# Base, expert and router products as one of 656 columns, with a new order of the stages

## The chip, the cores and the metric

The kernel runs on one core of a Trainium2 chip. The metric is the device time of one launch, in microseconds (us); lower is better.

## The reference

The input x has 128 batch rows of 32 x 512 floats. A block of four parts works on it: a mixing of the 32 rows of each batch entry by weights that depend on a condition, causal attention with grouped keys, a grouped convolution over the 512 positions, and a feed-forward part that adds eight low-rank experts, weighed by a router, to a base product.

```python
def _L0_cond_ref(x, embedding, W0, b0, W1, b1, W2, b2, weight, bias_k):
    ...
    out = jnp.einsum('boi,bih->boh', agg_w, x) + agg_b[:, :, None]
    return out
def _L0_attn_ref(x, Wq, Wk, Wv, Wo):
    ...
    scores = jnp.einsum('bkgqd,bkmd->bkgqm', qg, k) / np.sqrt(HEAD_DIM)
    scores = jnp.where(causal, scores, -jnp.inf)
    attn = jax.nn.softmax(scores, axis=-1)
    ...
    return out @ Wo
def _L0_ffn_ref(x, base_W, base_b, router_W, router_b, A, B, expert_map):
    ...
    base_out = jnp.einsum('btd,od->bto', x, base_W) + base_b
    logits = jnp.einsum('btd,nd->btn', x, router_W) + router_b
    probs = jax.nn.softmax(logits, axis=-1)
    topk_p, topk_i = jax.lax.top_k(probs, E)
    mapped = expert_map[topk_i]
    onehot = (mapped[..., None] == jnp.arange(E)).astype(x.dtype)
    w = jnp.einsum('btk,btke->bte', topk_p, onehot)
    h = jnp.einsum('btd,erd->bter', x, A)
    lora = jnp.einsum('bter,eor->bto', h * w[..., None], B) * SCALING
    return base_out + lora
...
    x = x + _L0_attn_ref(_L0_cond_ref(x, ...), ...)
    x = x + _L0_ffn_ref(_L0_cond2_ref(x, ...), ...)
```

## The kernel before

Four batch rows make a group of 128 partitions; there are G = 32 groups. All engines run one program of steps t, one step for each group, and in each step every engine works on groups of different age: `live(t)` guards the attention of group t, `live(t - 1)` its output projection, the convolution and the router's input, `live(t - 2)` the base product and the experts, `live(t + 1)` the mixing of the next group. The first steps and the last are written out (`peeled`), the middle ones are one loop. Each engine takes its instructions in the order in which `steps` writes them; between engines there are only semaphores. So the order is a hand-written one, and a wait in front of an instruction holds up all that follows on that engine.

The names that the text uses, in the order of TensorE (PE) in a step: `qkv` (12 products of 512 columns for the queries, 12 of 256 for keys and values), `project` (12 of 512, the output projection of the group before), `transpose_qk`, `base` (12 of 512 into PSUM bank 6), `transpose_hw` and `lora` (the expert part: 3 of 512, added into bank 6), `scores`, `conv` (12 products of 128 columns, in full fp32, two records each in the trace), `transpose_p`, `mix` (bank 6), `values` (reads what ScalarE copies out of the transposes, tile `prT`, by the name `raw` in the trace), `heads` (12 of 256 columns, of which 143 are used: 128 for the experts' inner products, 15 for the router), `transpose_o`. Three products stand where one would do mathematically, since each fp32 operand is split into a high and a low part of type fp32r: high x high, high x low, low x high. In the trace the 36 products of `qkv` and `project` and the 12 of `heads` all carry line L375, that of the helper `product`.

VectorE (DVE) does the rope, the key tile (`keys`, L974), x1 = attention + input (L1016), half of the copies by phase for the convolution (L282; ScalarE does the others), the row maximum and its subtraction for the softmax (L983, L985, in two halves h), the output sum (L1042), the convolution's bias (`zs`, L1048), the mixing's bias (`ys`, L1060), the router (`route`, `route2`, 12 small instructions) and the normalisation of the attention (L992, L994). ScalarE (ACT) makes the high parts and the exponentials, GpSimd (POOL) the low parts `z_lo` (L786) and `y_lo`, and x1 + bias (`x1b`, L800).

Of the kernel before, what the change touches and what calls it, by code (L numbers as in the profile page):

```python
# [34 lines left out]
NAR = 256  # L35
# [51 lines left out]
def build(nc, x, cond, fside, cW0, cb0, cW1, cb1, cW2, cb2, cweight, cbias, Wq, Wk, Wv, Wo,  # L87
          convw, convc, baseW, baseb, routerW, routerb, loraA, loraB, emap, const, out):
    with ExitStack() as ctx:
# [17 lines left out]
        base_hi = sb("base_hi", [P, PH, D], F32R)  # L107
        base_lo = sb("base_lo", [P, PH, D], F32R)
        ar_hi = sb("ar_hi", [P, PH, NAR], F32R)
        ar_lo = sb("ar_lo", [P, PH, NAR], F32R)  # L110
# [149 lines left out]
        ffn_ps, out_sb = sem("ffn_ps"), sem("out_sb")  # L260
# [8 lines left out]
        def iterate(eng, steps):  # L269

            for t in range(-1, 3):
                steps(t)
            with eng.Fori(3, G - 1) as t:
                steps(t)
            for t in range(G - 1, G + 2):
                steps(t)
# [11 lines left out]
        def _(sp):  # L288
# [55 lines left out]
            def steps(t):  # L344
# [4 lines left out]
                if live(t - 2):  # L349
                    wait(sp, out_sb, t - 1)  # L350
                    sp.dma_start(group(out_g, t - 2), outS).then_inc(out_st, 16)
# [5 lines left out]
            for t in range(-1, 3):  # L357
                steps(t)
            with sp.Fori(3, G - 2) as t:
                steps(t)  # L360
            for t in range(G - 2, G + 2):
                steps(t)
# [3 lines left out]
        def _(pe):  # L366
# [97 lines left out]
            def mix(u):  # L464
# [10 lines left out]
            def qkv(t):  # L475
                pe.wait_ge(y_hi_sb, t + 1)
                pe.wait_ge(y_lo_sb, t + 1)

                wait(pe, sx_sb, 2 * t)
                y = [(y_hi[:, c * P:(c + 1) * P], y_lo[:, c * P:(c + 1) * P]) for c in range(KC)]  # L480
                if peeled(t, 0):
# [4 lines left out]
                        ).then_inc(q_ps, 1)  # L486
                if peeled(t, 0):
# [19 lines left out]
            def transpose_hw(u):  # L507
                pe.wait_ge(hw_sb, u + 1)
                nc.tensor.transpose(ps[:, 7, 0:P], hw[:, :, :].rearrange("p e r -> p (e r)"), ident).then_inc(hwT_ps, 1)

            def base(u):
                z = [(z_hi[:, j, :], z_lo[:, j, :]) for j in range(PH)]
                n = 0
                for j in range(PH):
                    for a, b in ((z_hi, base_hi), (z_hi, base_lo), (z_lo, base_hi)):
                        mm(ps[:, 6, :], a[:, j, :], b[:, j, :], start=(n == 0), stop=False)  # L516
                        n += 1
# [13 lines left out]

            def lora(u):
                pe.wait_ge(hwT_hi_sb, u + 1)
                pe.wait_ge(hwT_lo_sb, u + 1)
                mm(ps[:, 6, :], hwT_hi[:, :], lora_hi[:, :], start=False, stop=False)  # L535
                mm(ps[:, 6, :], hwT_hi[:, :], lora_lo[:, :], start=False, stop=False)  # L536
                mm(ps[:, 6, :], hwT_lo[:, :], lora_hi[:, :], start=False, stop=True).then_inc(ffn_ps, 1)  # L537
# [18 lines left out]
            def values(t):  # L556

                wait(pe, zs_sb, t)
# [8 lines left out]
            def heads(u):  # L567

                pe.wait_ge(z_hi_sb, u + 1)
                pe.wait_ge(z_lo_sb, u + 1)  # L570
                z = [(z_hi[:, j, :], z_lo[:, j, :]) for j in range(PH)]
                product(ps[:, 7, 0:NAR], z, [(ar_hi[:, j, :], ar_lo[:, j, :]) for j in range(PH)]).then_inc(ar_ps, 1)

            def transpose_o(t):
                pe.wait_ge(on_sb, t + 1)

                wait(pe, ys_sb, t + 2 if live(t + 1) else 0)
                for b in range(NB):
                    last = nc.tensor.transpose(ps[:, 6, b * P:(b + 1) * P], on[:, b, :], ident)  # L579
# [518 lines left out]
```

## Time and profile before

| | |
|---|---|
| median of 3 runs | 747.89 us (747.72 to 748.15) |
| profiled execution | 748.08 us, of which the span of the trace is 746.1 us |
| TensorE busy | 711.7 us, 95% of the span |
| VectorE busy | 543.9 us, 73% |
| ScalarE busy | 272.5 us, 37% |
| GpSimd busy | 147.6 us, 20% |
| DMA | 47 GB/s over the span |

The span is the time from the first to the last instruction on the slowest (here the only) core. Busy time of TensorE is that of its matmul records, which overlap; so a busy share near 100% tells that the engine is rarely idle, and the distance from one start to the next tells what a matmul costs. PEld is TensorE's weight load, which runs beside the matmuls.

### The profile page before, as it was taken

The page shows a single profiled execution, that of the slowest core. Times are in us where ns is not written, and L with a number is a line of the kernel's source. Part 1 is how long each engine was busy: PE and PEld are TensorE (multiplying, and loading weights), DVE is VectorE, ACT ScalarE, POOL GpSimd, SP SyncE. Part 2 cuts the span into 40 slices and gives each one's busy share as a digit, 9 for nine tenths or more (in the row PEclk, how much of TensorE's full clock was granted, in tenths as well). Part 3 has the DMA queues.
Part 4 walks back from the last instruction along what each step waited for, and adds up shares of the span by engine and source line. Part 5 has one row for each costly group of instructions (what it writes and reads, how often), then busy time and mean ns, then how long its engine had stood idle before and what let it go on. Part 6 is the DMA issues. An engine that isn't in the chain of part 4 may idle for free.

```text
span 746.1 us, 13077 instructions
## 1 busy us (share of the span) xinstructions
PE 711.7 (95%) x4478; PEld 628.5 (84%) x4510; DVE 543.9 (73%) x1424; ACT 272.5 (37%) x635; POOL 147.6 (20%) x116
## 2 busy tenths in 40 slices
PE   5879999999999999999999999999999999999985
PEld 4578888888888888888888888888889888888874
DVE  5457787777778777777877777788777777877763
ACT  4135433333443333344333323433333344333331
POOL 5232201222221122222102222210122222012211
PEclk9979999999999999999999999999999999999999
DMA  7751100111110011111100111110011111001000
GB/s 189 169 242 29 43 17 27 42 42 42 42 42 31 15 38 42 42 42 42 40 16 28 42 42 42 42 42 14 28 42 42 42 42 42 19 23 42 29 29 29
DMA packets 27392, 35.43 MB, mean 47 GB/s; under 512 B 11651, under 2 KB 13347, under 8 KB 26998
## 3 DMA queue, kind: packets, MB, share of 16 engines
q1 hardware_dynamic: 26374, 34.88, 15.1%
q10 hardware_dynamic: 864, 0.14, 0.1%
q0 software_dynamic: 144, 0.28, 0.1%
q8 instruction: 6, 0.10, 0.1%
q14 instruction: 4, 0.03, 0.0%
HBM read 26.36 MB, written 8.93 MB: 47 GB/s over the span
## 4 chain that ended last, share of the span: by engine, by line
PE 82%; ACT 7%; POOL 5%; DVE 3%; issue 2%; DMA 0%; POOLq 0%; SPq 0%; DVEq 0%
PE ps L375 37%; PE ps L516 11%; PE ps L545 11%; PE ps L528 8%; POOL z_lo L786 5%; ACT raw L644 4%; PE ps L552 2%; PE ps L579 2%; ACT z_hi L644 2%; PE ps L504 2%; PE ps L562 1%; PE ps L535 1%; PE ps L536 1%; PE ps L537 1%; PE ps L526 1%
## 5 line engine op out<-in xcount | busy, mean ns | idle before, releaser
L786 POOL TENSOR_TENSOR z_lo<-raw,z_hi 128x512 fp32r<-128x512 f32 x32 | 40.8, 1274 | 561.1 <-ACT z_hi L644 561.1
L545 PEld LDWEIGHTS ps<-convW,x1ph 128*128 128x128 f32 x768 | 90.6, 192 | 2.8
L545 PE MATMUL ps<-convW,x1ph 128*128 128x128 f32 x768 | 90.9, 275 | 0.0
L644 ACT ACTIVATE x1ph<-raw 32x128 f32<-32x128 f32 x256 | 78.9, 308 | 32.0 <-DVE raw L1016 29.4
L375 PE MATMUL ps<-wqkv_hi,y_hi 128*128 128x512 f32 (+1 forms) x256 | 90.5, 353 | 0.0
L375 PE MATMUL ps<-wqkv_hi,y_lo 128*128 128x512 f32 (+1 forms) x256 | 87.4, 341 | 0.0
L375 PE MATMUL ps<-wqkv_lo,y_hi 128*128 128x512 f32 (+1 forms) x256 | 87.3, 341 | 0.0
L644 ACT ACTIVATE qk_t<-ps 128x512 f32<-128x512 f32 x32 | 19.1, 598 | 177.5 <-PE ps L505 177.5
L811 DVE TENSOR_TENSOR oT_lo<-ps,oT_hi 128x512 fp32r<-128x512 f32 x32 | 22.1, 692 | 70.8 <-ACT oT_hi L644 70.8
L528 PE MATMUL ps<-qk_t 128*128 128x256 f32 x256 | 66.7, 383 | 4.4 <-issue 2.8
L723 ACT ACTIVATE raw<-raw 128x512 f32<-128x512 f32 x64 | 40.3, 630 | 76.5 <-DVE raw L985 76.5
L562 PE MATMUL ps<-vm,raw 128*128 128x68 f32 x512 | 61.1, 273 | 0.3 <-ACT raw L644 0.3
L562 PEld LDWEIGHTS ps<-vm,raw 128*128 128x128 f32 x512 | 60.1, 193 | 0.6 <-DVE raw L1048 0.6
L282 DVE COPY x1ph<-raw 32x128 f32<-32x128 f32 x256 | 55.6, 217 | 3.0
L528 PEld LDWEIGHTS ps<-qk_t 128*128 128x128 f32 x256 | 49.3, 193 | 9.2 <-issue 0.3
L958 DVE TENSOR_TENSOR network<-ps,cst 128x512 f32<-128x512 f32 x64 | 31.5, 492 | 33.4 <-PE ps L375 33.0
L375 PEld LDWEIGHTS ps<-wqkv_hi,y_hi 128*128 128x128 f32 x256 | 49.3, 192 | 7.6 <-issue 1.5
L375 PEld LDWEIGHTS ps<-wqkv_lo,y_hi 128*128 128x128 f32 x256 | 49.1, 192 | 6.2
L375 PEld LDWEIGHTS ps<-wqkv_hi,y_lo 128*128 128x128 f32 x256 | 48.9, 191 | 6.2
L516 PE MATMUL ps<-base_hi,z_hi 128*128 128x512 f32 x128 | 53.0, 414 | 0.0
L375 PE MATMUL ps<-wo_hi,oT_hi 128*128 128x512 f32 x128 | 49.8, 389 | 1.6 <-DVE oT_lo L811 1.6
L516 PE MATMUL ps<-base_hi,z_lo 128*128 128x512 f32 x128 | 50.5, 395 | 0.0
(168 smaller groups left out, 1530.1 us busy)
## 6 DMA issues: line engine op xcount, KB each, us to landing
xm<-x SPq DMA_DIRECT2D x32, 256.0 KB, 2.6
xr<-x SPq DMA_DIRECT2D x32, 256.0 KB, 2.8
out<-raw SPq DMA_DIRECT2D x32, 256.0 KB, 2.0
convb<-convb_dram SPq DMA_DIRECT2D x1, 2048.0 KB, 12.2
mixb<-mixb_dram SPq DMA_DIRECT2D x1, 1792.0 KB, 8.7
raw<-L_attn_Wq SPq DMA_DIRECT2D x4, 256.0 KB, 4.0
raw<-L_attn_Wo SPq DMA_DIRECT2D x8, 128.0 KB, 4.5
raw<-L_ffn_base_W SPq DMA_DIRECT2D x1, 1024.0 KB, 5.8
```

The lines of the kernel that those rows point to most:

```text
L282: last = copy(x1ph[S * j:S * (j + 1), b, 1:P + 1], x1[S * b:S * (b + 1), j, :])
L375: last = mm(dst, a, b, start=(n == 0), stop=(n == 3 * len(left) - 1))
L504: nc.tensor.transpose(ps[:, 2, g * P:(g + 1) * P], qk[:, g * P:(g + 1) * P], ident)
L516: mm(ps[:, 6, :], a[:, j, :], b[:, j, :], start=(n == 0), stop=False)
L528: last = mm(ps[:, h, (b % 2) * 256:(b % 2) * 256 + 256], qT[:, b, :, :].rearrange("p g q -> p (g q)"), kT[:, b, :, :].rearrange("p k m -> ...
L545: last = mm(zo[:, :, b * S:(b + 1) * S], x1ph[:, b, s:s + P], convW[:, s, :, :], start=(s == 0), stop=(s == SHIFTS - 1))
L562: last = mm(ps[:, 4 + k // 4, (k % 4) * NB * VW:(k % 4 + 1) * NB * VW], prT[:, k, :], vm[:, k, :, :].rearrange("p b c -> p (b c)"), start= ...
L644: return nc.scalar.activation(dst, src, ACT.Copy)
L723: nc.scalar.activation(pr.rearrange("p (k b m) -> p b k m", k=NKV, b=NB)[:, 2 * h:2 * h + 2, :, :], sx.rearrange("p (b k m) -> p b k m", b ...
L786: nc.gpsimd.tensor_tensor(z_lo[:, :, :].rearrange("p j n -> p (j n)"), zs, z_hi[:, :, :].rearrange("p j n -> p (j n)").bitcast(F32), ALU.s ...
L811: return v.tensor_tensor(dst, value, hi.bitcast(F32), ALU.subtract)
L958: v.tensor_tensor(a, src, cst[:, C_COS:C_SIN].unsqueeze(1).broadcast_to([P, h, HD]), ALU.mult)
```

## The change

`base` and `heads` become one function `feed_forward`. For each of the 4 phases and 3 combinations of high and low parts it issues two products on the same weights, of 384 and of 272 columns: 656 in all, where there were 512 and 256. It now runs for the group t - 2, one half before `scores` and one half behind. `lora` runs one step later than before, for t - 3; since the 512 outputs now lie in two banks, it issues 384 and 128 columns in place of 512. The last 128 outputs of the base product stay in bank 7, whence VectorE adds them to x1b before the bank is used anew, and `lora` writes its 128 columns into bank 5. The output sum becomes two instructions. `mix` moves to bank 0, where the first half of the scores lies, and stands ahead of `conv`; the transposes of `on` move behind the queries, that of `hw` to the end of the step. The other engines' orders follow. All in all there is one more step at the end (the loops run to G + 3).

```diff
 NR = 2 * NE - 1
-NAR = 256
+NAR = 144
...
-        ar_hi = sb("ar_hi", [P, PH, NAR], F32R)
-        ar_lo = sb("ar_lo", [P, PH, NAR], F32R)
+        ffn_hi = sb("ffn_hi", [P, PH, D + NAR], F32R)
+        ffn_lo = sb("ffn_lo", [P, PH, D + NAR], F32R)
...
-                wait(pe, out_sb, u - 2)
+                wait(pe, sx_sb, 2 * u - 1)
                 for c in range(KC):
-                    last = mm(ps[:, 6, c * P:(c + 1) * P], xm[:, c * P:(c + 1) * P],
+                    last = mm(ps[:, 0, c * P:(c + 1) * P], xm[:, c * P:(c + 1) * P],
...
+            def lora(u):
+
+                pe.wait_ge(hwT_hi_sb, u + 1)
+                pe.wait_ge(hwT_lo_sb, u + 1)
+                for n, (a, b) in enumerate(((hwT_hi, lora_hi), (hwT_hi, lora_lo), (hwT_lo, lora_hi))):
+                    mm(ps[:, 6, 0:BASE6], a[:, :], b[:, 0:BASE6], start=False, stop=(n == 2))
+                    last = mm(ps[:, 5, 0:P], a[:, :], b[:, BASE6:D], start=(n == 0), stop=(n == 2))
+                last.then_inc(ffn_ps, 1)
+
...
+            def feed_forward(u, phases):
+
+                for j in phases:
+                    for n, (a, b) in enumerate(((z_hi, ffn_hi), (z_hi, ffn_lo), (z_lo, ffn_hi))):
+                        first, final = j == 0 and n == 0, j == PH - 1 and n == 2
+                        mm(ps[:, 6, 0:BASE6], a[:, j, :], b[:, j, 0:BASE6], start=first, stop=False)
+                        last = mm(ps[:, 7, 0:P + NAR], a[:, j, :], b[:, j, BASE6:D + NAR], start=first, stop=final)
+                return last
...
+                wait(pe, x1_sb, t)
                 wait(pe, zs_sb, t)
...
-                    qkv(t)
+                    queries(t)
+                if live(t - 1):
+                    transpose_o(t - 1)
+                if live(t):
+                    keys_values(t)
...
+                if live(t - 3):
+                    lora(t - 3)
...
                 if live(t - 2):
-                    base(t - 2)
-                    transpose_hw(t - 2)
+                    pe.wait_ge(z_hi_sb, t - 1)
+                    pe.wait_ge(z_lo_sb, t - 1)
+                    wait(pe, out_sb, t - 2)
+                    feed_forward(t - 2, (0, 1))
                 if live(t):
                     scores(t)
                 if peeled(t, 1):
                     prepare_base((2, 3))
                 if live(t - 2):
-                    lora(t - 2)
-                if live(t - 1):
-                    conv(t - 1)
-                if live(t):
-                    transpose_p(t)
+                    feed_forward(t - 2, (2, 3)).then_inc(ar_ps, 1)
...
                 if live(t + 1):
                     mix(t + 1)
...
+                if live(t - 1):
+                    conv(t - 1)
+                if live(t):
+                    transpose_p(t)
+                if peeled(t, 0):
+                    pe.wait_ge(prep_sb, 2)
                 if live(t):
                     values(t)
-                if live(t - 1):
-                    heads(t - 1)
-                if live(t):
-                    transpose_o(t)
+                if live(t - 2):
+                    transpose_hw(t - 2)
...
-                if live(t - 2):
-                    route(t - 2)
-                if live(t):
-                    rope(t)
-                if live(t - 2):
-                    route2(t - 2)
+                if live(t):
+                    rope(t, 1, qkv_ps, D, P)
+                    roped(t)
+                if live(t - 3):
+                    dve.wait_ge(ffn_ps, t - 2)
+                    dve.wait_ge(last_sb, t - 2)
+
+                    wait(dve, out_st, 16 * (t - 3))
+                    out3 = outS.rearrange("p (n j) -> p j n", j=PH)
+                    v.tensor_tensor(out3[:, 0:3, :], ps[:, 6, 0:BASE6].rearrange("p (j n) -> p j n", j=3), x1b[:, 0:3, :], ALU.add)
+                    v.tensor_tensor(out3[:, 3, :], ps[:, 5, 0:P], x1b[:, 3, :], ALU.add).then_inc(out_sb, 1)
+                if live(t):
+                    keys(t)
                 if live(t - 1):
...
-                    minus(hwT_lo[:, :], ps[:, 7, 0:P], hwT_hi[:, :]).then_inc(hwT_lo_sb, 1)
...
+                if live(t - 2):
+                    route(t - 2)
+                    dve.wait_ge(x1b_sb, t - 1)
+                    v.tensor_tensor(x1b[:, 3, :], ps[:, 7, 0:P], x1b[:, 3, :], ALU.add).then_inc(last_sb, 1)
...
+                if live(t - 2):
+                    route2(t - 2)
```

On ScalarE the copy of the transposed `hw` moves to the start of the step, the router's copy `arS` between the two exponentials, and y_hi ahead of the copies for `values`:

```diff
+                if live(t - 3):
+                    act.wait_ge(hwT_ps, t - 2)
+                    copy(hwT_hi[:, :], ps[:, 1, 0:P]).then_inc(hwT_hi_sb, 1)
...
+                for h in range(2):
+                    if live(t):
...
+                    if h == 0 and live(t - 2):
+                        act.wait_ge(ar_ps, t - 1)
+                        copy(arS[:, :], ps[:, 7, P:P + NAR]).then_inc(ar_sb, 1)
+                if live(t + 1):
+                    act.wait_ge(ys_sb, t + 2)
+                    copy(y_hi[:, :], ys[:, :]).then_inc(y_hi_sb, 1)
...
+                if live(t - 2):
+                    act.wait_ge(lgs_sb, t - 1)
+                    nc.scalar.activation(ex[:, :], lgs[:, :], ACT.Exp).then_inc(ex_sb, 1)
```

On GpSimd x1b is now made for the group t - 2, behind the output sum of t - 3:

```diff
+                if live(t - 2):
...
+                    wait(pool, out_sb, t - 2)
+                    nc.gpsimd.tensor_tensor(x1b, x1, basebB[:, :].rearrange("p (n j) -> p j n", j=PH),
+                                            ALU.add).then_inc(x1b_sb, 1)
```

TensorE before, in the loop, from the last product of `base` to the convolution (L528 are the scores, L535 to L537 `lora`, L545 `conv`):

```order
L516 MATMUL ps<-base_hi,z_lo 128x512
L508 REGISTER_ALU
L509 MATMUL ps<-cst,hw 128x128
L526 MATMUL ps<-causal16,ident16 128x512
L528 MATMUL ps<-qk_t 128x256 x2
L526 MATMUL ps<-causal16,ident16 128x512
L528 MATMUL ps<-qk_t 128x256 x2
L535 MATMUL ps<-lora_hi,hwT_hi 128x512
L536 MATMUL ps<-lora_lo,hwT_hi 128x512
L537 MATMUL ps<-lora_hi,hwT_lo 128x512
L545 MATMUL ps<-convW,x1ph 128x4x32 x12
```

TensorE now, at the scores of the same loop (L528 and L529 are the pair of `feed_forward`, L541 the scores), to the mixing (L471) and the convolution (L551):

```order
L529 MATMUL ps<-ffn_hi,z_lo 128x272
L539 MATMUL ps<-causal16,ident16 128x512
L541 MATMUL ps<-qk_t 128x256 x2
L539 MATMUL ps<-causal16,ident16 128x512
L541 MATMUL ps<-qk_t 128x256 x2
L528 MATMUL ps<-ffn_hi,z_hi 128x384
...
L467 ISA
L85 ISA
L471 ISA
L471 MATMUL ps<-mixw,xm 128x128 x4
L551 MATMUL ps<-convW,x1ph 128x4x32 x12
```

The transpose of `hw` and `lora` are gone from here, half of the merged products stands behind the scores, and `mix` stands before `conv`.

TensorE before, at the end of the loop (L552 is `transpose_p`, L470 `mix`, L562 `values`, L375 the first of `heads`):

```order
L552 MATMUL ps<-cst,raw 128x128 x8
L466 ISA
L470 ISA
L470 MATMUL ps<-mixw,xm 128x128 x4
L561 REGISTER_ALU
L562 MATMUL ps<-vm,raw 128x68 x4
L561 REGISTER_ALU
L562 MATMUL ps<-vm,raw 128x68 x4
L375 MATMUL ps<-ar_hi,z_hi 128x256
```

TensorE now, at the end of the loop (L558 is `transpose_p`, L569 `values`, L577 the transpose of `hw`):

```order
L551 MATMUL ps<-convW,x1ph 128x4x32 x12
L558 MATMUL ps<-cst,raw 128x128 x8
L568 ISA
L569 MATMUL ps<-vm,raw 128x68 x4
L568 REGISTER_ALU
L569 MATMUL ps<-vm,raw 128x68 x4
L577 MATMUL ps<-cst,hw 128x128
```

Nothing stands any more between `transpose_p` and `values`, and `heads` no longer follows `values`.

VectorE now, in the loop, from the output sum of group t - 3 (L1032, L1033) over `keys` (L987) and x1 (L1041) to the softmax and `ys` (L1059):

```order
L1032 TENSOR_TENSOR raw2<-ps,raw2 128x3x128
L1033 TENSOR_TENSOR raw2<-ps,raw2 128x128
L987 TENSOR_TENSOR qk_t<-ps,cst 128x1024
L1038 REGISTER_ALU
L85 REGISTER_ALU
L1041 TENSOR_TENSOR raw2<-ps,xr 128x512
L283 COPY x1ph<-raw2 32x128 x8
L993 ISA
L996 TENSOR_REDUCE mx<-ps 128x16
L998 TENSOR_TENSOR raw<-ps,mx 128x512
```

Before, x1 stood ahead of `keys` and the output sum behind the softmax; now the key tile is followed by x1, the copies by phase and the softmax without a gap.

## Rows read from the trace of the kernel before

**Rows 1.** The page: busy time of TensorE, its share and instructions.

```profile
PE 711.7 (95%) x4478; PEld 628.5 (84%) x4510; DVE 543.9 (73%) x1424; ACT 272.5 (37%) x635; POOL 147.6 (20%) x116
```

**Rows 2.** Chain of waits, one step of the loop: start us, length us, what.

```profile
403.02 2.80 PE ps L516 x12
...
405.92 0.05 issue
...
408.78 2.68 PE ps L545 x24
...
413.69 1.28 POOL z_lo L786
...
415.10 1.65 PE ps L375 x12
...
424.65 2.79 PE ps L516 x12
```

**Rows 3.** Timeline of TensorE from `values` to `heads`: start, length us.

```profile
348.16 1.90 PE L562 MATMUL ps<-vm,raw 128*128 128x68 f32 x16
350.20 0.36 PE L375 MATMUL ps<-ar_hi,z_hi 128*128 128x256 f32 x1
350.39 0.28 PE L375 MATMUL ps<-ar_lo,z_hi 128*128 128x256 f32 x1
...
351.57 0.28 PE L375 MATMUL ps<-ar_hi,z_lo 128*128 128x256 f32 x1
```

**Rows 4.** Timeline, step 31, which has no `mix`: transposes, copies, `values`.

```profile
714.16 1.04 PE L552 MATMUL ps<-cst,raw 128*128 128x128 f32 x8
...
714.80 1.09 ACT L644 ACTIVATE raw<-ps 128x512 f32<-128x512 f32 x2 [0.93 <-PE ps L552]
715.54 1.97 PE L562 MATMUL ps<-vm,raw 128*128 128x68 f32 x16 [0.34 <-ACT raw L644]
```

**Rows 5.** Timeline of VectorE: key tile to softmax, and x1 alone.

```profile
339.50 1.22 DVE L974 TENSOR_TENSOR qk_t<-ps,cst 128x1024 f32<-128x1024 f32 x1
340.63 1.83 DVE L282 COPY x1ph<-raw 32x128 f32<-32x128 f32 x8
...
342.70 0.68 DVE L983 TENSOR_REDUCE mx<-ps 128x16 f32<-128x512 f32 x1
343.42 0.69 DVE L985 TENSOR_TENSOR raw<-ps,mx 128x512 f32<-128x512 f32 x1
...
724.65 1.08 DVE L1016 TENSOR_TENSOR raw<-ps,xr 128x512 f32<-128x512 f32 x1 [0.53 <-PE ps L375]
```

**Rows 6.** Timeline of the first steps, and from the chain the start of step 3.

```profile
30.05 0.27 PE L505 MATMUL ps<-cst,qk 128*128 128x128 f32 x1
...
30.36 1.23 DVE L974 TENSOR_TENSOR qk_t<-ps,cst 128x1024 f32<-128x1024 f32 x1 [1.88 <-PE ps L505]
...
39.01 1.91 PE L470 MATMUL ps<-mixw,xm 128*128 128x128 f32 x8
...
46.66 1.12 PE L579 MATMUL ps<-cst,raw 128*128 128x128 f32 x4 [3.80 <-DVE raw L994]
47.43 0.78 PE L375 MATMUL ps<-wqkv_hi,y_hi 128*128 128x512 f32 x1
...
92.69 6.91 PE ps L375 x36
```

**Rows 7.** Chain of waits in the last steps: start us, length us, what.

```profile
730.02 2.69 PE ps L545 x24
...
737.32 0.40 ACT arS L644
...
740.53 0.34 PE ps L509
...
742.62 1.06 DVE raw L1042
```

More of the change, by code:

```diff
@@ L269, in iterate @@
         def iterate(eng, steps):
-            for t in range(-1, 3):
+            for t in range(-1, 4):
                 steps(t)
-            with eng.Fori(3, G - 1) as t:
+            with eng.Fori(4, G - 1) as t:
                 steps(t)
-            for t in range(G - 1, G + 2):
+            for t in range(G - 1, G + 3):
                 steps(t)
@@ L355, in steps @@
                     sp.dma_start(xm[:, :], group(x_g, t + 2)).then_inc(xm_in, 16)
-            for t in range(-1, 3):
+            for t in range(-1, 4):
                 steps(t)
-            with sp.Fori(3, G - 2) as t:
+            with sp.Fori(4, G - 2) as t:
                 steps(t)
-            for t in range(G - 2, G + 2):
+            for t in range(G - 2, G + 3):
                 steps(t)
@@ L473, in mix, with queries @@
                 last.then_inc(y_ps, 1)
-            def qkv(t):
+            def queries(t):
                 pe.wait_ge(y_hi_sb, t + 1)
                 pe.wait_ge(y_lo_sb, t + 1)
-                wait(pe, sx_sb, 2 * t)
                 y = [(y_hi[:, c * P:(c + 1) * P], y_lo[:, c * P:(c + 1) * P]) for c in range(KC)]
@@ L486, in qkv, with keys_values @@
                         ).then_inc(q_ps, 1)
+            def keys_values(t):
+                if live(t - 3):
+                    pe.wait_ge(hwT_hi_sb, t - 2)
+                    pe.wait_ge(hwT_lo_sb, t - 2)
+                y = [(y_hi[:, c * P:(c + 1) * P], y_lo[:, c * P:(c + 1) * P]) for c in range(KC)]
                 if peeled(t, 0):
@@ L505, in transpose_qk @@
                 nc.tensor.transpose(ps[:, 3, 0:P], qk[:, D:D + P], ident).then_inc(qT_ps, 1)
[L507 to L517, printed above, removed]
+            def feed_forward(u, phases):
[5 more added lines that the diff above has]
+                return last
             def scores(t):
@@ L565, in values, with transpose_hw, transpose_o @@
                         last.then_inc(o_ps, 1)
[L567 to L577, printed above, removed]
+            def transpose_hw(u):
+                pe.wait_ge(hw_sb, u + 1)
+                nc.tensor.transpose(ps[:, 1, 0:P], hw[:, :, :].rearrange("p e r -> p (e r)"), ident).then_inc(hwT_ps, 1)
+            def transpose_o(u):
+                pe.wait_ge(on_sb, u + 1)
                 for b in range(NB):
-                    last = nc.tensor.transpose(ps[:, 6, b * P:(b + 1) * P], on[:, b, :], ident)
+                    last = nc.tensor.transpose(ps[:, 4, b * P:(b + 1) * P], on[:, b, :], ident)
                 last.then_inc(oT_ps, 1)
@@ L714, in steps @@
                     by_phase(copy, (1, 3)).then_inc(ph_act, 1)
-                if live(t - 2):
-                    act.wait_ge(hwT_ps, t - 1)
-                    copy(hwT_hi[:, :], ps[:, 7, 0:P]).then_inc(hwT_hi_sb, 1)
                 if peeled(t, 1):
                     prepare_base((2, 3))
-                if live(t):
-                    for h in range(2):
+                for h in range(2):
+                    if live(t):
                         act.wait_ge(sx_sb, 2 * t + 1 + h)
@@ L999, in steps @@
             def steps(t):
+                if live(t - 3):
+                    dve.wait_ge(hwT_hi_sb, t - 2)
+                    minus(hwT_lo[:, :], ps[:, 1, 0:P], hwT_hi[:, :]).then_inc(hwT_lo_sb, 1)
+                if live(t):
+                    rope(t, 0, q_ps, 0, D)
                 if live(t - 1):
```

126 lines of the change are left out of this document (49 added, 77 removed).

## The prediction

> **What bounds the kernel now.** I read the page first: TensorE is busy 95% of the span [rows 1], so what counts is what its instructions cost and the few places where it waits. Next the chain of waits inside the loop: nearly all of a step lies on TensorE, and a step takes 424.65 - 403.02 = 21.63 us [rows 2]. The only other piece of weight is one visit to ScalarE and GpSimd: z_lo, 1.28 us, after which `heads` can begin 0.14 us later [rows 2]. Third the timeline there, for what that visit costs TensorE: 16 records of `values` start 0.108 us apart ((1.90 - 0.28) / 15), so they need 1.73 us, yet `heads` starts 2.04 us after them: 0.31 us of waiting. The first product of `heads` then takes 0.19 us where the later ones are 0.118 us apart ((351.57 - 350.39) / 10), another 0.07 us [rows 3]. With 0.05 us around the transpose of `hw` [rows 2] a step holds 0.43 us in which TensorE does nothing. The rest is work.
>
> **The merged products.** `base` is 12 products of 512 columns in 2.80 us, 0.233 us each [rows 2]; those of 256 are 0.118 us apart [rows 3]. The line through the two gives 0.45 ns for a column, so 384 columns cost 0.176 us and 272 cost 0.125 us, a pair 0.301 us, twelve pairs 3.61 us. Before it was 2.80 + 1.41 = 4.21 us. **Term 1: -0.60 us a step.** It could be -0.56 (112 columns less at the 2.4 GHz that the page grants) to -0.64.
>
> **lora in two banks.** Before: 3 products of 512, 0.70 us. Now 3 of 384 (0.53 us) and 3 of 128. No row shows an fp32r product of fewer than 256 columns. From below it is bounded by the weight load that each product has: records of 128 columns with a load each never start closer than 2.68 / 24 = 0.112 us in `conv` [rows 2]. From above by what a whole product of 128 columns costs in `conv`, which is full fp32 and takes two such records: 0.223 us. So lora is 0.86 or 1.20 us, **term 2: +0.16 or +0.50 us**. I take the upper end: `conv` is the only row with this many columns in a product, and that fp32r is cheap is shown from 256 columns on only. I hold this to be about 2 to 1, and the sign of the whole hangs on it.
>
> The Trainium skill ("TensorE: Matmul & The Clock Gate", sections "LDWEIGHTS" and "Back-to-back issue gap") gives columns / 1.2 ns for a weight load and N / 2.4 + 2.5 ns for the gap of a matmul, with nothing special for few columns; that would be 107 ns and 56 ns here, so the load would set the pace and lora would be the cheap case. Its gap for 512 columns, 216 ns, is below the 233 ns of this trace.
>
> **Waits taken away.** z_lo is now needed one step later (feed_forward of t - 2), so the 0.31 + 0.07 us go. The transpose of `hw` stands at the end of the step, the 0.05 us go too. **Term 3: -0.43 us.** In its new place the transpose needs `route2`, which VectorE does behind the bias of the convolution; by my walk it is done 2.8 us after the start of `transpose_p`, and TensorE arrives at 3.1 us, so nothing is lost, with 0.3 us in hand.
>
> **A wait put in front of values.** `mix` stood between `transpose_p` and `values` and covered ScalarE's first copy of the transposes. The last step but two of the kernel before has no `mix`, and shows what is left without it: transposes at 714.16, first copy at 714.80, `values` at 715.54, that is 1.38 us after the transposes' start, where eight transposes alone need 0.88 us ((1.04 - 0.27) / 7 each) [rows 4]. **Term 4: +0.50 us in every step.**
>
> **A wait put in front of mix.** `mix` now writes bank 0 and waits for the first half of the softmax's subtraction. Counted from the start of the merged products: VectorE's key tile starts 0.04 us after the last transpose ends [rows 6], that is at 0.20; x1 follows 1.13 us later (340.63 - 339.50), takes 1.08 + 0.04 us, the eight copies 1.83 + 0.03 us, maximum and subtraction of half a tile 343.42 + 0.69 - 342.70 = 1.41 us [rows 5], and TensorE restarts 0.14 us behind [rows 2]: 5.86 us. TensorE itself is there after 3.61 us of pairs and 2.11 us of scores (405.97 to 408.08, which is `conv`'s start less `lora`) [rows 2]: 5.72 us. **Term 5: +0.14 us**, and it means that cheaper pairs than I assume would give nothing: VectorE's chain sets this stretch.
>
> **At no cost, by what covers it.** oT_lo is ready some 0.3 us before `project`, because `lora` stands in front of it. The output sum (two instructions, by length of L1042 about 0.87 and 0.40 us, in place of 1.06) ends 0.8 us before `feed_forward` asks for it. x1b on GpSimd starts behind that sum and must be over before x1 is rewritten: 0.5 us in hand. The extra addition of 128 columns falls where VectorE waits for `conv`. y_lo is ready 2.5 us before the queries.
>
> **A step** so changes by -0.60 + 0.50 - 0.43 + 0.50 + 0.14 = +0.11 us, to 21.74 us; with the cheap lora by -0.23 us.
>
> **The start.** Before, TensorE is idle for 3.80 us until the normalised attention of group 0 is there, and starts the queries of step 1 at 47.43 [rows 6]. Now the queries stand ahead of those transposes. TensorE was free at 46.66 - 3.80 = 42.86; `mix` (1.91 us, 39.01 [rows 6]) now fills an idle stretch ahead of the transposes, against which VectorE's preparations come later and give 0.6 us back: queries at 41.7, 5.7 us earlier. Steps 1 and 2 took 92.69 - 47.43 = 45.26 us [rows 6], so step 1 took 23.63. Now step 2 lacks lora (group 0 comes to it in step 3): 20.54 us. Step 1 runs no `heads` and no transposes of `on` (1.9 us), but `mix` and `conv` now wait behind VectorE's chain, so I give it 23.4 us. Step 3 starts at 85.6 instead of 92.7: **-7.1 us**, of which some 3 us is work that only comes later.
>
> **Steps 3 to 31:** 29 x 0.11 = **+3.2 us**; the last of them has no `mix` and no wait for it, **-1.0 us**.
>
> **The end.** Before, the loop ends at 92.69 + 29 x 21.63 = 720.0, `conv` of the last group starts at 730.02 and ends at 732.7, and the span ends 13.4 us later [rows 7]; the router of the last group runs while `base` runs. Now `conv` ends at 12.4 us after the loop instead of 12.7. Behind it: bias and second half of the router of group 30 (2.6), transpose, high and low part (1.0), lora (1.6), output (1.2), only then may bank 6 be rewritten by the merged products of group 31 (4.0), then its whole router with nothing beside it (737.32 to 740.53 less the shorter copy [rows 7], 3.1), transpose and parts (1.0), lora (1.6), output (1.2), and 2.4 us from the output sum's end to the span's end (746.1 - 743.68 [rows 7]): 19.7 us. **+6.0 us.**
>
> **Sum:** -7.1 + 3.2 - 1.0 + 6.0 = +1.1 us on 748.08 us of the profiled execution, 0.19 us above the median: **749.0 us**, a rise of 0.15%. A measurement of this kernel tells about 0.2% (1.5 us) from no change, so this is at the edge of it. Errors of 0.1 us in a step make 3 us: own range 745 to 754.
>
> **Rivals.**
> (a) The 128-column products run at the pace of the weight load. Step -0.23 us: 29 x 0.23 = -6.7, end 0.7 us shorter: -7.1 - 6.7 - 1.0 + 5.3 = -9.5 us, **738.4 us**. For it: fp32r falls in proportion from 512 to 256 columns [rows 2, 3]. This is what the page's rule gives.
> (b) GpSimd's x1b lengthens VectorE's chain. It waits for the output sum and holds back x1, which holds back the copies, the softmax, `mix` and all behind. Margin 0.5 us; from there on each 0.1 us is 3 us in all. If the output sum waits for lora and rope longer than I walked it and x1b ends 0.7 us later, a step costs 0.2 us more: **755 us**. For it: x1b runs beside VectorE's key tile now; against it: today's z_lo and y_lo also run beside VectorE work without harm.
> (c) The waits of terms 4 and 5 are partly work's own time: half of them gone would be -0.32 us x 29, **740 us**, a third gone 743. Against it: row 4 shows the first directly.
>
> **Chances.** The forecast 0.56, of which 0.24 slower, 0.20 within 0.2%, 0.12 faster, since its value is next to the bound; (a) 0.24, faster; (b) 0.12, slower; (c) 0.08, faster. Together faster 0.44, same 0.20, slower 0.36. The range takes in (a) and (b) and the scatter about them on the near side: 737 to 756.
>
> **What would show it.** Right: pairs of 384 and 272 columns 0.30 us together; products of 128 columns in lora 0.22 us apart from the next; `values` 1.38 us behind the transposes' start; `mix` waiting for L998; a step of 21.7 us; queries of step 1 near 42; some 33 us from the last loop step's end to the span's. Wrong: a step of 21.4 with lora's short products 0.11 us apart (a); VectorE idle before x1 with GpSimd as releaser (b); `values` earlier than 1.3 us (c); or a waiting place in the loop that I don't list, above all the transpose of `hw`, which has only 0.3 us in hand.

## The result, and the profile after

The changed kernel takes 800.3 us (median; 796.78 to 804.93) where the kernel before takes 747.95 us in the same session: ratio 1.070, 95% interval 1.065 to 1.076. It is 7% slower; the forecast of 749.0 us, and its range of 737 to 756, are missed by a wide margin. The profiled execution took 804.93 us, with a span of 802.6 us.

The page of the changed kernel, the rows that answer to [rows 1], then the granted clock and the chain by engine:

```profile
PE 741.0 (92%) x4606; PEld 654.6 (82%) x4606; DVE 578.9 (72%) x1488; ACT 263.6 (33%) x635; POOL 148.8 (19%) x116
...
PEclk9889999999999999999999999999999999999996
...
PE 80%; DVE 15%; issue 2%; ACT 1%; DMA 0%; DVEq 0%; SPq 0%
```

TensorE is busy for 29 us more though it has fewer columns to stream, and VectorE is on the chain with 15% of the span, where it had 3% before. A table of stretches, cut at the starts of `ys` (now L1059), shows a step each: stretch, its length, busy time and count of TensorE, weight loads, VectorE, ScalarE and GpSimd, granted clock, DMA.

```profile
88.05:109.58 21.53, 21.19 (x144) 19.18 (x143) 16.47 (x45) 7.72 (x19) 4.18 (x3) 1.00 0.13 38
...
131.36:154.19 22.83, 21.76 (x144) 19.41 (x143) 17.54 (x45) 7.72 (x20) 4.06 (x3) 1.00 0.12 34
...
177.11:201.47 24.36, 23.31 (x144) 20.56 (x143) 17.53 (x45) 7.74 (x20) 4.09 (x3) 0.93 0.11 32
```

So there are three kinds of step. The first two (21.53 and 21.78 us) are close to the forecast of 21.74 us. From the third on VectorE is busy 1.03 to 1.07 us longer and the step takes 22.84 us; and 10 of the 28 steps between the starts of `ys` at 88.05 and 740.15 take 24.34 us at a mean granted clock of 0.93. Against 21.63 us that makes 16 x 1.21 + 10 x 2.71 = 46.5 us, most of the 56.9 us between the profiled executions. The rest: step 3 begins 1.0 us later than before, and about 9 us are lost after the loop.

The stretch below lies among the queries of the first slow step. The granted clock is 0.50 there, that is, the lower level, 1.2 GHz:

```profile
184.59:187.15 2.56, 2.56 (x8) 1.98 (x7) 0.17 (x1) 0.00 (x0) 0.00 (x0) 0.50 0.00 0
```

The chain of waits through one of the steps of 22.84 us, which answers to [rows 2] (start us, length us, what):

```profile
411.30 2.69 PE ps L551 x24
414.13 0.69 DVE raw L1081
...
416.19 1.43 DVE hw L958
417.67 0.33 PE ps L577
418.00 0.24 issue
418.23 3.05 PE ps L376 x12
```

z_lo and `heads` are gone from it, as intended, and in their place the chain runs through the bias of `conv`, the router's second half and `hw` (the experts' inner products times their weights) to the transpose that now ends the step. One link is out of proportion: `hw` takes 1.43 us. The timeline there, and the same place in the first full step, where the step was not long (start, length, in brackets the idle time before it and its releaser, the instruction that it waited for):

```profile
416.19 1.42 DVE L958 SCALAR_TENSOR_TENSOR hw<-arS,exR,we 128x128 f32<-128x128 f32 x1
416.20 1.27 POOL L810 TENSOR_TENSOR z_lo<-raw,z_hi 128x512 fp32r<-128x512 f32 x1 [2.04 <-ACT z_hi L655]
417.67 0.33 PE L577 MATMUL ps<-cst,hw 128*128 128x128 f32 x1 [0.56 <-DVE hw L958]
```

```profile
92.71 0.35 DVE L958 SCALAR_TENSOR_TENSOR hw<-arS,exR,we 128x128 f32<-128x128 f32 x1
92.84 1.36 POOL L810 TENSOR_TENSOR z_lo<-raw,z_hi 128x512 fp32r<-128x512 f32 x1 [2.08 <-ACT z_hi L655]
...
93.64 0.27 PE L577 MATMUL ps<-cst,hw 128*128 128x128 f32 x1
93.67 0.48 PE L376 MATMUL ps<-wqkv_hi,y_hi 128*128 128x512 f32 x1
```

When `hw` starts 0.13 us ahead of GpSimd's z_lo it takes 0.35 us; when both start together it ends 0.14 us after z_lo has ended. Such an instruction, longer because GpSimd is at work, is called held in what follows. It shows in its own length and not as idle time, so the views of waits name `hw` and never z_lo. Over the whole run (fastest, median, slowest in ns, then who waited for it: us, times):

```profile
L958 DVE SCALAR_TENSOR_TENSOR hw<-arS,exR,we x32: 351/1416/1424, 92.7 to 795.6; 128x128 f32<-128x128 f32 x32
...
  PE ps L577: 21.3, 29
```

In the kernel before it took 0.352 to 0.353 us all 32 times, with z_lo at another place. The Trainium skill ("SBUF — State Buffer", section "Who interferes with whom") has a rule for this: a VectorE instruction with two SBUF inputs and a GpSimd instruction that reads SBUF exclude each other for a whole instruction, as a copy or cast in a two-port mode and a GpSimd instruction do, and the one that issues first wins. With that rule the trace agrees, with 1.42 against 0.35 us; I had not applied it. Which of the two issued first can't be read from starts 0.01 us apart: the record of `hw` begins at 416.19, that of z_lo at 416.20, and yet `hw` is the one held.

### The profile page after: what moved, and what is told of

It reads as the page before. It is cut to its first block, busy times and chain, and to the rows that moved or that the text cites. A ratio compares the mean times of both kernels' runs of the same rounds, so it can differ in the third digit from the quotient of the medians.

```text
span 802.6 us, 13318 instructions
## 1 busy us (share of the span) xinstructions
PE 741.0 (92%) x4606; PEld 654.6 (82%) x4606; DVE 578.9 (72%) x1488; ACT 263.6 (33%) x635; POOL 148.8 (19%) x116
## 4 chain that ended last, share of the span: by engine, by line
PE 80%; DVE 15%; issue 2%; ACT 1%; DMA 0%; DVEq 0%; SPq 0%
PE ps L376 31%; PE ps L551 11%; PE ps L528 8%; PE ps L541 7%; PE ps L529 6%; DVE hw L958 5%; PE ps L471 5%; PE ps L506 3%; DVE raw L1081 2%; PE ps L539 2%; PE ps L583 2%; PE ps L520 2%; PE ps L577 1%; DVE selE L953 1%; DVE we L956 1%
## 5 line engine op out<-in xcount | busy, mean ns | idle before, releaser
L376 PE MATMUL ps<-wqkv_hi,y_hi 128*128 128x512 f32 (+1 forms) x256 | 99.3, 388 | 6.2 <-issue 6.2
L799 POOL TENSOR_TENSOR raw<-raw,basebB 128x512 f32<-128x512 f32 x32 | 49.3, 1540 | 274.3 <-DVE raw L1033 274.3
L376 PE MATMUL ps<-wqkv_lo,y_hi 128*128 128x512 f32 (+1 forms) x256 | 93.4, 365 | 0.0
L376 PE MATMUL ps<-wqkv_hi,y_lo 128*128 128x512 f32 (+1 forms) x256 | 93.0, 363 | 0.0
L551 PE MATMUL ps<-convW,x1ph 128*128 128x128 f32 x768 | 92.6, 278 | 0.1
L551 PEld LDWEIGHTS ps<-convW,x1ph 128*128 128x128 f32 x768 | 89.9, 195 | 0.4 <-ACT x1ph L655 0.4
L803 POOL TENSOR_TENSOR y_lo<-ys,y_hi 128x512 fp32r<-128x512 f32 x31 | 39.4, 1271 | 274.0 <-ACT y_hi L655 274.0
L569 PEld LDWEIGHTS ps<-vm,raw 128*128 128x128 f32 x512 | 59.6, 191 | 16.2 <-ACT raw L655 13.2
L569 PE MATMUL ps<-vm,raw 128*128 128x68 f32 x512 | 63.9, 278 | 8.7 <-ACT raw L655 8.1
L376 PEld LDWEIGHTS ps<-wqkv_hi,y_hi 128*128 128x128 f32 x256 | 53.2, 208 | 17.9 <-issue 12.1
L541 PE MATMUL ps<-qk_t 128*128 128x256 f32 x256 | 67.5, 387 | 0.0
L987 DVE TENSOR_TENSOR qk_t<-ps,cst 128x1024 f32<-128x1024 f32 x32 | 39.2, 1224 | 39.2 <-PE ps L521 39.2
L655 ACT ACTIVATE oT_hi<-ps 128x512 fp32r<-128x512 f32 x32 | 19.1, 598 | 125.8 <-PE ps L583 125.8
L376 PEld LDWEIGHTS ps<-wqkv_hi,y_lo 128*128 128x128 f32 x256 | 52.8, 206 | 7.4
L376 PEld LDWEIGHTS ps<-wqkv_lo,y_hi 128*128 128x128 f32 x256 | 53.1, 207 | 5.7
L541 PEld LDWEIGHTS ps<-qk_t 128*128 128x128 f32 x256 | 50.1, 196 | 9.3 <-issue 0.3
```

The costliest lines, as they stand in the source:

```text
L376: last = mm(dst, a, b, start=(n == 0), stop=(n == 3 * len(left) - 1))
L541: last = mm(ps[:, h, (b % 2) * 256:(b % 2) * 256 + 256], qT[:, b, :, :].rearrange("p g q -> p (g q)"), kT[:, b, :, :].rearrange("p k m -> ...
L551: last = mm(zo[:, :, b * S:(b + 1) * S], x1ph[:, b, s:s + P], convW[:, s, :, :], start=(s == 0), stop=(s == SHIFTS - 1))
L569: last = mm(ps[:, 4 + k // 4, (k % 4) * NB * VW:(k % 4 + 1) * NB * VW], prT[:, k, :], vm[:, k, :, :].rearrange("p b c -> p (b c)"), start= ...
L655: return nc.scalar.activation(dst, src, ACT.Copy)
L799: nc.gpsimd.tensor_tensor(x1b, x1, basebB[:, :].rearrange("p (n j) -> p j n", j=PH), ALU.add).then_inc(x1b_sb, 1)
```

## The experiments

Ratios are to the kernel before, timed on the same chip in the same session.

### e1: z_lo waits for hw

```diff
                 if live(t - 1):
+                    if live(t - 2):
+                        pool.wait_ge(hw_sb, t - 1)
                     pool.wait_ge(zs_sb, t)
```

> GpSimd makes z_lo only after VectorE has written hw; nothing else changes. Theory 'held by GpSimd': hw (L958) takes 1.42 us in a step only because it starts together with z_lo, and it goes back to 0.35 us; TensorE no longer waits at the end of the step, the loop's branch is hidden again, no step falls to the low clock; a step of 21.4 to 21.6 us, total 738 to 744. Rival 'the instruction is slow in this place for another reason': hw stays at 1.42 us, step 22.8, total 795 to 805.

758.7 us, ratio 1.013 (1.011 to 1.016): one wait on GpSimd gives back 41.6 of the 52.3 us (800.3 less 758.7, 800.3 less 748.0). The timeline:

```profile
461.38 0.35 DVE L960 SCALAR_TENSOR_TENSOR hw<-arS,exR,we 128x128 f32<-128x128 f32 x1
...
461.81 1.29 POOL L812 TENSOR_TENSOR z_lo<-raw,z_hi 128x512 fp32r<-128x512 f32 x1 [2.47 <-DVE hw L960]
```

Steps in the loop are 21.73 to 21.79 us, all at clock 1.00: both the long `hw` and the slow steps are gone. The expected total, 738 to 744 us, was missed by 15 us all the same: the step is not the 21.4 to 21.6 us that I counted on, and what is lost at the start and at the end (e6 and e7) was not in it.

### e2: hw reads PSUM

```diff
-                v.scalar_tensor_tensor(hw[:, :, :], arS[:, 0:P].rearrange(
+                v.scalar_tensor_tensor(hw[:, :, :], ps[:, 7, P:2 * P].rearrange(
```

> hw reads the experts' products from PSUM bank 7 instead of their copy in SBUF; it still starts together with z_lo. Theory 'only an instruction with all operands in SBUF is held by GpSimd': hw 0.3 to 0.5 us, step 21.4 to 21.6, total 738 to 744. Rival 'any VectorE instruction is held while GpSimd works': hw stays near 1.4 us, total 795 to 805.

757.1 us, ratio 1.012 (1.008 to 1.015). Here z_lo does lie beside `hw`:

```profile
459.47 0.35 DVE L958 SCALAR_TENSOR_TENSOR hw<-ps,exR,we 128x128 f32<-128x128 f32 x1
459.49 1.27 POOL L810 TENSOR_TENSOR z_lo<-raw,z_hi 128x512 fp32r<-128x512 f32 x1 [2.04 <-ACT z_hi L655]
...
460.23 0.28 PE L577 MATMUL ps<-cst,hw 128*128 128x128 f32 x1
```

The same instruction with one large operand moved from SBUF to PSUM isn't held. So it is not GpSimd's work as such that costs, but where VectorE reads from. The length of `hw` is as expected, the total is again above the 738 to 744 us, for the same reasons.

### e3: the transpose of hw behind the next queries

```diff
                     queries(t)
+                if live(t - 3):
+                    transpose_hw(t - 3)
                 if live(t - 1):
                     transpose_o(t - 1)
...
-                if live(t - 2):
-                    transpose_hw(t - 2)
...
-                nc.tensor.transpose(ps[:, 1, 0:P], hw[:, :, :]
+                nc.tensor.transpose(ps[:, 7, 384:512], hw[:, :, :]
```

> The transpose of hw moves from the end of the step behind the queries of the next one, into unused columns of bank 7, and its low part behind the first half of the rope. hw stays slow (1.42 us), but TensorE does not wait for it. Theory 'the cost is TensorE's wait at the loop's end': step 21.5 to 21.8 (some 0.2 us new wait in front of lora or project), no low clock, total 740 to 750. Rival 'the collision costs by itself, through VectorE': above 22.3 us a step.

757.1 us, ratio 1.010 (1.008 to 1.013). `hw` is held as before, but nobody waits for it:

```profile
460.04 1.44 DVE L955 SCALAR_TENSOR_TENSOR hw<-arS,exR,we 128x128 f32<-128x128 f32 x1
460.05 1.28 POOL L807 TENSOR_TENSOR z_lo<-raw,z_hi 128x512 fp32r<-128x512 f32 x1 [2.04 <-ACT z_hi L652]
460.76 0.48 PE L376 MATMUL ps<-wqkv_hi,y_hi 128*128 128x512 f32 x1
```

TensorE has gone on to the queries while `hw` still runs. Steps are 21.65 to 21.67 us at clock 1.00, as expected; the total is above the expected 740 to 750 us by what start and end lose. Three different ways to take the held instruction off the end of the step come out within 1.6 us of each other, so its wait, with the low clock that follows, accounts for 42 to 43 us of the loss.

### e5: the same wait without GpSimd

```diff
+                for n in range(3):
+                    v.scalar_tensor_tensor(idle[n][:, :, :], arS[:, 0:P].rearrange(...), exR[:, :], ...)
                 v.scalar_tensor_tensor(hw[:, :, :], arS[:, 0:P]...
```

An earlier form of this run, e4, with `hw` computed four times into its own tile, gave no time.

> As e1 (z_lo waits for hw, so that nothing of GpSimd lies beside hw), but VectorE computes the same result three more times into tiles that nobody reads, ahead of the one that counts. 3 x 0.35 us make the transpose of hw about as late as the held instruction of the changed kernel does (1.42 us), with no instruction of GpSimd in it. Theory (a wait of TensorE of this length once a step brings the low clock, whoever causes it): undisturbed steps of 22.8 us, stretches of steps near 24.3 us at a mean granted clock of 0.93, together 795 to 805 us. Rival (the low clock comes with the collision of the two engines, not with the wait): the granted clock stays at 1.00 in the loop, all steps are 22.8 us, together 758.7 + 29 x 1.05 = 789 us.

800.0 us (796.3 to 804.6), ratio 1.071 (1.067 to 1.074), the time of the changed kernel. Stretches between starts of `ys`:

```profile
154.86:178.99 24.13, 23.32 (x144) 20.65 (x143) 17.25 (x48) 7.75 (x20) 4.08 (x3) 0.93 0.10 33
178.99:201.53 22.54, 21.77 (x144) 19.44 (x143) 17.25 (x48) 7.75 (x20) 4.09 (x3) 1.00 0.11 35
```

```profile
413.40 0.33 PE L578 MATMUL ps<-cst,hw 128*128 128x128 f32 x1 [0.28 <-DVE hw L964]
413.96 0.73 PE L377 MATMUL ps<-wqkv_hi,y_hi 128*128 128x512 f32 x1 [0.24 <-issue]
```

`hw` itself takes 0.343 to 0.347 us. So the low clock needs neither z_lo beside `hw` nor a held instruction; a wait of TensorE at the end of each step brings it. The wait is not quite the one that was aimed at: 0.28 us ahead of the transpose where the changed kernel has 0.56, with the same 0.24 us behind it, so the undisturbed step is 22.54 us and not 22.8, and even this shorter wait brings the low clock. That the two totals agree to 0.3 us is partly chance. Not every step is a slow one: 8 are in the profiled execution here and 10 in that of the changed kernel, two or three in a row each time, and why these and not others is left open.

### e6: convW in step 1

```diff
                     roped(t)
+                if peeled(t, 1):
+                    pad_conv()
...
                     prepare_conv()
-                    prepare_experts()
                 if peeled(t, 1):
                     prepare_base((2, 3))
+                    prepare_experts()
```

`pad_conv` holds the twelve copies that stood in `prepare_conv` on VectorE.

> On top of e3. The twelve small copies into convW, which in iteration 0 lie beside GpSimd's y_lo and wo_lo and take 7.3 us instead of 1.8, move to iteration 1 behind the roped queries and keys, where GpSimd is idle; the expert map moves behind the softmax of iteration 1. Theory (these held copies are what makes the normalised attention of group 0 late, for which TensorE waits 4.7 us, and what the start lost against my forecast): copies 1.8 us, TensorE's wait ahead of the first transposes of on gone or under 1 us, project about 5 us earlier, together 757.1 - 5 = 752 us (750.5 to 754). Rival (GpSimd's own work, wo_lo, is as late for project): TensorE waits as long ahead of project instead, gain under 2 us, 755.5 to 757 us.

752.2 us, ratio 1.006 (1.004 to 1.008), 4.9 us under e3 by the medians, 6.5 by the spans (756.1 and 749.6). The timeline of the start, in the changed kernel, which answers to [rows 6]:

```profile
40.10 7.36 DVE L903 COPY convW<-cvT 32x32 f32<-32x32 f32 x12
41.12 6.02 POOL L787 TENSOR_TENSOR wo_lo<-raw,wo_hi 128x512 fp32r<-128x512 f32 x4 [0.71 <-ACT wo_hi L655]
...
41.57 0.48 PE L376 MATMUL ps<-wqkv_hi,y_hi 128*128 128x512 f32 x1
...
49.53 1.12 PE L583 MATMUL ps<-cst,raw 128*128 128x128 f32 x4 [4.92 <-DVE raw L1007]
```

and in e6:

```profile
41.28 6.07 POOL L784 TENSOR_TENSOR wo_lo<-raw,wo_hi 128x512 fp32r<-128x512 f32 x4 [0.97 <-ACT wo_hi L652]
...
44.50 0.60 PE L580 MATMUL ps<-cst,raw 128*128 128x128 f32 x4
...
47.45 0.47 PE L376 MATMUL ps<-wo_hi,oT_hi 128*128 128x512 f32 x1 [0.96 <-POOL wo_lo L784]
...
48.55 1.80 DVE L902 COPY convW<-cvT 32x32 f32<-32x32 f32 x12
```

Twelve copies of SBUF into SBUF take 1.80 us alone and 7.36 us beside GpSimd; the normalised attention stands behind them, and TensorE waits for that. With them gone GpSimd's wo_lo is the next limit, by 0.96 us only. Step 3 begins at 85.99 us, where the forecast had 85.6.

### e7: banks of its own for the last group

```diff
+                b6, b7 = (0, 1) if last_group(u) else (6, 7)
...
+                if last_group(t - 2):
+                    feed_forward(t - 2, (0, 1))
                 if live(t - 3):
                     lora(t - 3)
```

> On top of e3. The merged products of the last group go to banks 0 and 1, which are free by then, and half of them stand ahead of lora of the group before; so they needn't wait until the output of that group has left banks 6 and 7. Theory (the end is long because two groups go through banks 6 and 7 one after the other): these products start at the end of z_lo, near 735.6 instead of 740.1, run at 2.4 GHz instead of 1.2 GHz (3.7 instead of 6.0 us), and the span ends 6 to 7 us earlier: 750.5 us (749.5 to 752). Rival (VectorE's route of the group before is what the last group waits for): under 3 us.

754.7 us (752.3 to 755.4), ratio 1.007 (1.004 to 1.009), 2.5 us under e3 by the medians and 3.7 us by the spans: between the two expectations. The timeline:

```profile
736.09 0.47 PE L581 MATMUL ps<-cst,hw 128*128 128x128 f32 x1 [3.07 <-DVE hw L966]
736.22 0.67 PE L532 MATMUL ps<-ffn_hi,z_hi 128*128 128x384 f32 x1
```

The products no longer wait for the output of group 30, but I had kept its transpose of `hw` ahead of them, and VectorE is still the one waited for, 3.07 us; the first four of the twelve pairs then run at 1.2 GHz (0.55 us a pair, the first 0.69). The theory was right about the banks and wrong that they were all of it.

### e8: e6 and e7 together

> e6 and e7 together. Theory: both add up, 757.1 - 5 - 6.5 = 745.5 us (744 to 747.5), ratio to the kernel before 0.995 to 0.999; steps of 21.66 us as in e3, so the loop itself is no faster than before. Rival (the ends of both overlap or a step in the loop takes the slack): 748 us or more.

749.1 us, ratio 1.0005 (0.999 to 1.002): the same as before. That is the number of the rival (748 us or more) but not its reason: the parts add up roughly (757.1 - 4.9 - 2.5 = 749.7), and 745.5 had counted on more from e7. With the losses found at the start and at the end taken back in part, the change still gives nothing, since a step is 21.66 us where it was 21.63.

### e9: the merged products whole, mix behind conv

```diff
-                    feed_forward(t - 2, (0, 1))
+                    feed_forward(t - 2, (0, 1, 2, 3)).then_inc(ar_ps, 1)
                 if live(t):
                     scores(t)
...
+                if live(t - 1):
+                    conv(t - 1)
...
                 if live(t + 1):
                     mix(t + 1)
...
-                if live(t - 1):
-                    conv(t - 1)
```

The diff shows only part of TensorE's order; the queries, VectorE, ScalarE and GpSimd have new orders too, as the expectation tells.

> On top of e8, with the aim to take back what the loop of e3 and e8 loses against the products' own lengths: there the merged products stand in two halves around the scores and each half starts anew (1.90 + 2.08 us for twelve pairs of 0.30), and mix stands ahead of conv, where it waits for VectorE. Now all twelve pairs stand ahead of the scores, conv follows the scores, and mix follows conv; the products with y_lo come last among the queries and alone wait for it; VectorE's route and bias of conv come ahead of ys, ScalarE's y_hi behind the copies of the transposes, z_lo waits for hw. Theory (restarts and the wait ahead of mix are what ate the 0.60 us of columns): a step of 21.45 us instead of 21.66 (21.35 to 21.55), together 749.1 - 29 x 0.21 = 743 us (740 to 746). Rival (y_hi and y_lo, now behind the longer way of mix, are late for the queries): a new wait ahead of the queries, a step of 21.8 to 22.3 us, 753 to 768 us, more with the low clock.

743.2 us (741.9 to 746.3), ratio 0.9925 (0.990 to 0.995), as expected and the first version below the kernel before, by 0.75%. A step, then the end of one in the timeline:

```profile
425.77:447.27 21.50, 21.16 (x143) 19.38 (x143) 17.47 (x45) 7.65 (x20) 4.10 (x3) 1.00 0.12 37
```

```profile
449.30 1.27 POOL L815 TENSOR_TENSOR y_lo<-ys,y_hi 128x512 fp32r<-128x512 f32 x1 [10.97 <-ACT y_hi L667]
449.33 1.39 DVE L974 SCALAR_TENSOR_TENSOR hw<-arS,exR,we 128x128 f32<-128x128 f32 x1
...
450.08 0.48 PE L490 MATMUL ps<-wqkv_hi,y_hi 128*128 128x512 f32 x1
```

Steps are 21.50 us. Several things were changed at once, so no run says what each of them gives. `hw` is held here too, now by y_lo, and it costs nothing, since its transpose comes after the queries.

## Why the prediction was wrong

**The step that failed** is the one on the transpose of `hw`: "it is done 2.8 us after the start of `transpose_p`, and TensorE arrives at 3.1 us, so nothing is lost, with 0.3 us in hand". Without the collision this holds within 0.1 us: in e2 the transposes start at 457.11, `hw` ends at 459.82 (2.71 us later) and TensorE is there at 460.23 (3.12 us). But I took `hw` at its old 0.35 us at a place where z_lo starts with it. In the changed kernel the transposes start at 413.82 and it ended at 417.61, 3.79 us later. The prediction did name this transpose as the place to watch, but gave its failure neither a price nor a chance. The reason that I gave under rival (b), that "today's z_lo and y_lo also run beside VectorE work without harm", was read too quickly: the VectorE work beside them reads PSUM (the normalisation, L992 and L994). A two-input instruction on SBUF beside GpSimd was in the trace of before, once, at the very start:

```profile
12.25 2.52 POOL L760 TENSOR_TENSOR wqkv_lo<-raw,wqkv_hi 128x512 fp32r<-128x512 f32 x2 [2.38 <-ACT wqkv_hi L644]
...
12.79 0.86 DVE L856 TENSOR_TENSOR convb<-attT,cbiasS 8x128 f32<-8x128 f32 x1
```

It has 128 elements a partition, like `hw`, takes 0.86 us, and ends at 13.65 us, just after the first of the two on GpSimd (at 12.25 + 1.28 us). That row was the warning, though no row shows how long it takes alone.

**What followed from it.** 1.07 us more for `hw` make a step 22.84 us where e2 has 21.75, 1.09 us more. Of these 0.73 us are the transpose's delay; the other 0.35 us come behind it: the queries start 0.56 us after the transpose, in e5 too, against 0.21 us in e2 and 0.03 us in the written-out step 3. The profile puts 0.24 us of this down to issue, and it appears only inside the loop; that it is the loop's turn, the jump back to its first instruction, is my reading, no run shows it alone. Then the clock: 10 steps x 1.5 us = 15 us, which e5 shows to come with a wait there. I had no term for the clock at all.

**Term 1** (-0.60 us) was right in its columns: in the chain a pair is 0.17 + 0.13 us = 0.30 us. The two halves start anew after the transposes and after the scores. At the second start the first product takes 0.36 us from 408.07 to 408.43 where later ones take 0.17. That is 0.19 us more, of which 0.10 us only look like a cost: this product begins 0.68 us after the last group of scores (407.39), where in the kernel before `lora` began 0.78 us after it (450.32 to 451.10). The other 0.09 us are what `lora` paid in this place before (0.32 us for its first product instead of 0.23). In e9, with one start, the twelve pairs begin at 437.53 and the last product at 441.09, which with its own 0.12 us makes 3.68 us.

**Term 2** (+0.50 us) was mis-sized, by my choice of the upper bound; it measured +0.17. The timeline of lora:

```profile
400.34 0.39 PE L506 MATMUL ps<-lora_lo,hwT_hi 128*128 128x384 f32 x1
400.57 0.22 PE L507 MATMUL ps<-lora_lo,hwT_hi 128*128 128x128 f32 x1
400.63 0.39 PE L506 MATMUL ps<-lora_hi,hwT_lo 128*128 128x384 f32 x1
400.85 0.22 PE L507 MATMUL ps<-lora_hi,hwT_lo 128*128 128x128 f32 x1
400.91 0.45 PE L376 MATMUL ps<-wo_hi,oT_hi 128*128 128x512 f32 x1
```

A product of 128 columns has the next one 0.06 us behind it, but that next one then takes longer: 0.23 us for 384 columns instead of 0.17, and 0.29 us for the first 512 of `project` instead of 0.23. So a pair takes 0.29 us (400.34 to 400.63), which is the 0.176 + 0.112 us of the lower bound, where one product of 512 columns took 0.233. All six take 0.81 us (400.10 to 400.91), and with the 0.06 us that `project` pays for the last of them 0.87, against the 0.86 of the lower bound and 0.70 before. Rival (a) was right here, in its price too. That the 0.06 us are a weight load that a short product can't cover is my reading; they fit it, and no run tests it alone.

**Term 3**: the wait for z_lo did go; the hand-over it was exchanged for is told above. **Term 4** (+0.50): `values` starts 1.29 us after the transposes where it was 0.88, +0.41 us. **Term 5**: `mix` starts 5.96 us after the merged products (404.19 to 410.15); forecast 5.86. Both are right within 0.1 us.

So even with cheap lora and without the collision the step is 21.66 to 21.75 us, not the 21.40 of rival (a). That e1 and e2 come out at the forecast's 21.74 us is luck: `lora` costs 0.33 us less than I took, and about as much lies in costs for which I had no term. Comparing e3's step with one of the kernel before in the two timelines (439.10 to 460.76 and 436.73 to 458.37), start to start: merged products -0.40, the former wait between `values` and `heads` -0.24, transpose of `hw` and scores -0.10; against that the copies ahead of `values` +0.41, `mix` +0.10, keys and values, lora and project together +0.23 (the short products of lora, and a first product behind transposes), the rest +0.02. A product that follows another kind of work pays such a restart four times a step before (`heads`, queries, `base`, `lora`) and four times in e3 (queries, keys and values, both halves), so their number did not grow. The gain was there; it went above all into the copies ahead of `values` and into lora's short products, and the merged products kept the restart behind the scores and got 0.08 us of waiting ahead of `mix`. e9 has neither of these last two, and its step is 0.16 us shorter; by the lengths in the trace they account for it.

**The start** (-7.1 us) came out as +1.0. The queries of step 1 stand at 41.57, forecast 41.7; what was missed is for the most part the same collision, between the copies into convW and wo_lo. Step 3 begins at 93.67 us, in e3 at 92.44, and in e6, without that collision, at 85.99 (forecast 85.6).

**The end** (19.7 us behind `conv`): 22.5 us, 780.13 to 802.6. The order that I walked is the one that happened; the chain shows what was longer:

```profile
780.17 0.69 DVE raw L1081
...
782.22 0.93 DVE hw L958
783.20 0.34 PE ps L577
...
786.80 0.66 PE ps L528
...
792.94 0.30 ACT arS L655
```

The merged products take 6.1 us instead of 4.0, since most of them run at 1.2 GHz behind the waits, and `hw` is held once more. The last row is ScalarE's copy of the router's sums, the answer to 737.32 in [rows 7]: there `base` still ran beside what follows, here nothing does, as forecast.

## What to carry to other kernels

When an instruction moves, look at what the other engines do at its new place and at where each of the two reads. In these runs a duration read at the old place held at the new one only where no GpSimd instruction that reads SBUF lay beside a VectorE instruction with two SBUF inputs, or beside copies from SBUF to SBUF; otherwise count up to one whole GpSimd instruction more, unless there is slack for it. Where TensorE's margin ahead of a hand-over is smaller than that, place the hand-over elsewhere (e3), order the two (e1), or read from PSUM (e2). And a saving in columns counts only net of the waits, restarts and short products that the new order makes: a product cut into 384 and 128 columns costs more than one of 512.

## What the runs showed of the hardware

- A VectorE instruction of 0.35 us took 1.42 us beside a GpSimd instruction of 1.27 us, and 0.35 us if it started 0.13 us earlier or read one of its large operands from PSUM. A small one was held alike: the router's first addition, 15 columns, 0.62 us instead of 0.17 beside x1b at 737.66 in e8. Twelve copies from SBUF to SBUF took 7.36 us beside GpSimd and 1.80 us alone.
- In the changed kernel TensorE stands still for 0.56 us ahead of the last transpose and for 0.24 us behind it, once in 22.8 us, and in 10 of 28 steps the mean granted clock fell to 0.93. In the first of them eight of the twelve queries behind that wait ran at 1.2 GHz (0.43 us a product instead of 0.23). With 0.28 us in place of the 0.56 (e5) it fell in 8 steps; with neither (e1 to e3) the granted clock of the loop's steps was 1.00.
- fp32r products of 272 columns took 0.125 us from start to start and those of 384 0.17 us, in proportion to 512 (0.233). Products of 384 and 128 columns in turn took 0.23 + 0.06 = 0.29 us, so a short one adds 0.11 us, double what its columns would cost by the same line, and as much as a record of 128 columns in `conv` (0.112 us).
- The first fp32r product behind transposes, `values` or scores takes 0.07 to 0.09 us more than behind its like: `heads` 0.19 and keys and values 0.20 instead of 0.12, queries and `lora` before 0.32 instead of 0.23.
